# An attention and expert-layer kernel on one core: work dealt out anew over the engines in four stages

## The chip, the cores and the metric

The kernel runs on one core of one Trainium2 chip. A core has TensorE (PE) for matmuls, VectorE (DVE), ScalarE (ACT) and GpSimd (POOL) for everything elementwise, and SyncE (SP), which here issues transfers. Each engine runs its own list of instructions in order, and the lists meet only at semaphores. The metric is the device time of one execution in microseconds (us), and less is better. The kernel before takes 305.31 us, the median of 3 runs (305.03 to 306.4).

## The reference

There are 4 batches of 1024 tokens with 128 features each, 4096 tokens in all. A layer norm without weights, attention without learned projections, a second layer norm and a layer of 8 experts of which each token uses 2:

```python
x = x + attention(layernorm(x))        # lhs = h*w_lhs, rhs = h*w_rhs
                                       # scores = lhs @ rhs.T; softmax; @ h
h = layernorm(x)                       # 4096 x 128
probs = softmax(h @ router_w.T)        # 8 experts
topk_probs, topk_idx = top_k(probs, 2)
topk_probs = topk_probs / sum(topk_probs)
y = gelu(h @ w_fc[e] + b_fc[e])        # 128 -> 512, for the 2 experts of a token
y = y @ w_proj[e] + b_proj[e]          # 512 -> 128
out = x + sum over the 2 experts of topk_probs * y
```

## The kernel before

A batch of 1024 tokens is two units of 512 and 8 tiles of 128 tokens; batches have the indices 0 to 3. The order of the work is written out by hand in five lists, one for each engine, and what an engine waits for is a count on a semaphore. Nothing is scheduled by a planner.

**Prologue.** DVE takes the moments of the first two units, POOL makes the reciprocal deviation and the shift (`scale`, L785), ACT writes the normalised rows of unit 0 (`normalise`, L967) and DVE those of unit 1 (L1689). PE turns them with an identity (`turn_h`, L1137), after and before matmuls that compute nothing and only keep it busy (`stay_busy`, L1127). ACT copies the turned rows rounded to the matmul's format (`high_parts`), and DVE computes what the rounding lost (`low_parts`, L1448). The parts with and without the weights are called q and hT.

**Attention.** For each batch there are 16 blocks of 128x512 scores, each from three matmuls of high and low parts (`score`, L1152). DVE takes the largest value of each row (`row_max`, L1503), PE adds its negative into the block (`turn_negs` L1164, `shift_scores` L1170), ACT takes the exponent (`exponent`, L991; a block whose bank is wanted is first copied aside by `keep_again`, L989), and PE multiplies with the rows (`attend`, L1182). Scores of batch b are mixed with the last exponents and products of batch b-1. Beside that DVE adds the attention's result, takes moments for the second norm (`take_stats2`, `take_moments2`), chooses experts (`picks`, `find_gap`) and finds each token's place among its expert's rows (`keep_ranks`, `find_slots`); ACT and DVE make the normalised rows in two half-precision parts (`make_h2` and `high_h2` on ACT, `split_h2` on DVE, L1572). POOL sends them by indirect DMA into `slots`, a list in DRAM that is sorted by expert: 16 transfers for each batch (`dispatch`, L838 and L846).

**Passage.** When the first two batches are in `slots`, the first tiles of the experts start while the last batches are still chosen and sent. A table that says which expert a tile belongs to is computed in steps (`make_table`, L455). Experts' work is cut into 47 tiles: 24 of 256 rows and 23 of 128 rows. `ORDER` (L69) lists them in the order in which they run. At step k, SP loads tile k from `slots` (L723), PE turns the rows of a coming tile, does the up matmuls of tile k (L1366 to L1368) and the down matmuls of tile k-2 (L1387), ACT copies (`copy_xT`, L1086) and takes gelu (L1094), DVE adds the bias and multiplies by the gate for tile k-3 (`add_bias` L1872, `gate` L1880) and reads the row numbers of tile k (`keep_rows`, L842). The last round of ranks is a matmul too (`rank_round`, L1199), at step 4, after the bias of tile 1.

**End.** POOL sends each result to its token's place in `results` (`give_back`, L950). SP loads the first half of `results` when the tiles before `EARLY` have been sent, and the second half after all; DVE adds both results of each token to the row (L1913, L1915), and the output is stored, from ACT's queue for the first half (L1123) and from SP's for the second. `NB` is 8 buffers of tiles, `NH` is 4 buffers of row numbers and results, `FULL` is 24.

## Time and profile before

| what | value |
|---|---|
| median of the runs | 305.31 us |
| profiled execution, its own time | 305.57 us |
| its span in the trace | 304.0 us |
| PE busy | 269.3 us, 89% |
| DVE busy | 229.5 us, 75% |
| ACT busy | 196.4 us, 65% |
| POOL busy | 180.6 us, 59% |

The 1.57 us between the profiled execution's time and its span lie around the traced instructions. A busy PE is not a PE at its peak, since matmuls are pipelined and their ends are modelled; a share is a mean over stages with different limits, so a stage has to be read by itself. The stages in the trace are: prologue until 12.3 us, attention of the four batches until 153.2, the passage with the first tiles until 210, tiles with nothing else beside them until 281, and the end until 304.

### The profile page before, as it was taken

The numbers are of one execution on the slowest core, as the hardware profiler recorded it, in microseconds if no ns is written. First come the engines' busy times: TensorE is split into PE (matmuls) and PEld (weight loads), VectorE is DVE, ScalarE is ACT, GpSimd is POOL, SyncE is SP. The second block draws the span as 40 slices with busy tenths as digits, with TensorE's granted clock in tenths as the row PEclk, the third lists the DMA queues.
The fourth block names the chain that finished last, engine by engine and source line by source line (L and its number), as shares of the span: only waits on it lengthen the run. The fifth ranks groups of instructions, "written<-read, shape, count | busy, mean of one in ns | idle before, by whom it ended". The sixth has DMA issues, their size and how long they took to land.

```text
span 304.0 us, 8244 instructions
## 1 busy us (share of the span) xinstructions
PE 269.3 (89%) x2223; PEld 240.0 (79%) x2223; DVE 229.5 (75%) x1002; ACT 196.4 (65%) x427; POOL 180.6 (59%) x245
## 2 busy tenths in 40 slices
PE   7999999899999988899999699998999999999400
PEld 3589998789978977678888589987999999998400
DVE  4699898979878868988989777794565556666736
ACT  2447378897359772545679947774788788898200
POOL 8111036017667792687877657777777777777600
PEclk9999999999999999999999999999999999999955
DMA  6960000000401100111251143124233332221986
GB/s 195 412 293 4 0 3 0 3 0 0 144 27 57 37 27 11 37 45 38 69 140 63 38 118 109 55 73 125 73 97 100 95 93 82 81 73 55 352 279 248
DMA packets 15450, 28.51 MB, mean 94 GB/s; under 512 B 3904, under 2 KB 9920, under 8 KB 15152
## 3 DMA queue, kind: packets, MB, share of 16 engines
q1 hardware_dynamic: 10224, 16.88, 17.0%
q0 software_dynamic: 4608, 10.07, 9.9%
q10 hardware_dynamic: 576, 1.05, 1.0%
q8 instruction: 20, 0.33, 0.5%
q14 instruction: 22, 0.18, 0.2%
HBM read 15.83 MB, written 12.16 MB: 92 GB/s over the span
## 4 chain that ended last, share of the span: by engine, by line
PE 50%; POOL 14%; issue 13%; DVE 9%; DMA 7%; ACT 5%; SPq 1%; POOLq 0%; DVEq 0%; ACTq 0%
PE av_ps L1387 15%; PE av_ps L1182 11%; POOL slots L846 10%; PE sc_ps L1366 4%; PE sc_ps L1368 3%; PE sc_ps L1367 3%; DVE neg_piece L1503 3%; DMA raw_proj<-results 3%; DMA slots<-stage,slot 2%; DMA slots_in<-slots 2%; PE bank L1353 2%; PE sc_ps L1171 2%; PE bank L1158 1%; ACT h_all L972 1%; PE bank L1160 1%
## 5 line engine op out<-in xcount | busy, mean ns | idle before, releaser
L1094 ACT ACTIVATE raw_fc<-sc_ps,bfc,scale_down 128x128 f32<-128x128 f32 (+1 forms) x188 | 81.6, 530 | 0.7 <-PE sc_ps L1368 0.7
L950 POOL DMA_INDIRECT results<-prob,result_row x71 | 68.6, 967 | 22.1 <-issue 12.2
L846 POOL DMA_INDIRECT slots<-stage,slot x64 | 64.1, 1002 | 29.2 <-issue 18.9
L1387 PE MATMUL av_ps<-raw_proj,raw_fc 128*128 x568 | 72.7, 278 | 2.8 <-issue 1.9
L1182 PE MATMUL av_ps<-h_all,prob 128*128 128x137 f32 x512 | 73.2, 285 | 0.6 <-DVE lg_part L1534 0.4
L1387 PEld LDWEIGHTS av_ps<-raw_proj,raw_fc 128*128 128x128 f32 x568 | 67.0, 192 | 4.9 <-issue 4.5
L1182 PEld LDWEIGHTS av_ps<-h_all,prob 128*128 128x128 f32 x512 | 66.8, 190 | 4.4 <-DVE res L1531 1.6
L1366 PE MATMUL sc_ps<-h_all,wfc_hi 128*128 128x128 f16 (+1 forms) x188 | 43.2, 247 | 1.3 <-ACT raw_fc L1094 1.2
L1872 DVE TENSOR_TENSOR h_all<-av_ps,bpr 128x256 f32<-128x256 f32 (+1 forms) x47 | 16.9, 359 | 35.4 <-PE sc_ps L1368 31.8
L1368 PE MATMUL sc_ps<-h_all,wfc_lo 128*128 128x128 f16 (+1 forms) x188 | 43.1, 246 | 0.0
L1367 PE MATMUL sc_ps<-h_all,wfc_hi 128*128 128x128 f16 (+1 forms) x188 | 43.1, 246 | 0.0
L1086 ACT ACTIVATE h_all<-bank 128x512 f16<-128x512 f16 (+1 forms) x47 | 23.4, 501 | 25.2 <-PE sc_ps L1368 25.0
L1503 DVE TENSOR_REDUCE neg_piece<-bank 128x1 f32<-128x512 f32 x32 | 22.0, 687 | 7.3 <-PE sc_ps L1171 3.5
L999 ACT ACTIVATE prob<-sc_ps 128x512 f32<-128x512 f32 x32 | 18.1, 599 | 10.0 <-PE sc_ps L1171 9.9
L989 ACT ACTIVATE again<-bank 128x512 f32<-128x512 f32 x16 | 9.6, 597 | 21.9 <-DVE neg_piece L1503 21.9
L1503 DVE TENSOR_REDUCE neg_piece<-sc_ps 128x1 f32<-128x512 f32 x32 | 21.9, 684 | 1.1 <-PE sc_ps L1160 1.0
L1366 PEld LDWEIGHTS sc_ps<-h_all,wfc_hi 128*128 x188 | 18.4, 98 | 3.0 <-issue 1.8
L1880 DVE TENSOR_SCALAR prob<-h_all,row_gate 128x128 f32<-128x128 f32 x71 | 19.5, 301 | 1.4
L1368 PEld LDWEIGHTS sc_ps<-h_all,wfc_lo 128*128 x188 | 18.4, 98 | 1.1
L1367 PEld LDWEIGHTS sc_ps<-h_all,wfc_hi 128*128 x188 | 18.4, 98 | 0.8
L1353 PE MATMUL bank<-ident,slots_in 128*128 128x128 f16 x142 | 15.3, 219 | 2.2 <-DMA slots_in<-slots 2.2
L1009 ACT ACTIVATE h<-res,shift,rstd 128x128 f32<-128x128 f32 x32 | 14.4, 487 | 3.9 <-POOL shift L811 3.7
(201 smaller groups left out, 523.4 us busy)
## 6 DMA issues: line engine op xcount, KB each, us to landing
slots_in<-slots SPq DMA_DIRECT2D x24, 132.0 KB, 2.2
raw_fc<-in_w_fc_dram SPq DMA_DIRECT2D x1, 2048.0 KB, 11.3
raw_proj<-in_w_proj_dram SPq DMA_DIRECT2D x1, 2048.0 KB, 15.5
res<-in_x_dram SPq DMA_DIRECT2D x3, 512.0 KB, 5.9
slots_in<-slots SPq DMA_DIRECT2D x23, 66.0 KB, 1.8
results<-prob,result_row POOLq DMA_INDIRECT x71, 2.3
slots<-raw_fc POOLq DMA_DIRECT2D x2, 528.0 KB, 4.1
slots<-stage,slot POOLq DMA_INDIRECT x64
```

What stands on the lines that cost most here:

```text
L846: pool.indirect_dma_start(out=slots[:, :], out_offset=bass.IndirectOffsetOnAxis(ap=slot[:, n, k:k + 1], axis=0), in_=stage[:, b % 2, t, :] ...
L950: pool.indirect_dma_start(out=results[:, :], out_offset=bass.IndirectOffsetOnAxis(ap=result_row[a][:, h:h + 1], axis=0), in_=gated[a][h], ...
L1086: act.activation(xT[:, a % NH, 0:n], bank[a % 2][:, :].bitcast(F16)[:, 0:n], ACT.Copy).then_inc(xT_made, 1)
L1094: ins = act.activation(hid[:, a % NH, c, 0:halves_of(k) * P], up_ps(k, c), ACT.Gelu_apprx_tanh, bias=bfc[:, e, c:c + 1], scale=scale_down[ ...
L1182: mm = pe.matmul(att[:, t, 0:AUG], probT[:, m % RING, t * P:(t + 1) * P], h_aug[:, b % 2, exp_rows(n), :], start=(n % BT == 0 and t % 2 == ...
L1353: mm = pe.transpose(o[:, part * w + h * P:part * w + (h + 1) * P], x, ident16[:, :])
L1366: pe.matmul(o, wfc_hi[:, e, of], xT[:, a % NH, 0:w], start=True, stop=False, skip_group_check=True)
L1367: pe.matmul(o, wfc_hi[:, e, of], xT[:, a % NH, w:2 * w], start=False, stop=False, skip_group_check=True)
L1368: mm = pe.matmul(o, wfc_lo[:, e, of], xT[:, a % NH, 0:w], start=False, stop=True, skip_group_check=True)
L1387: mm = pe.matmul(o, hid[:, a % NH, c, rows], wpr[:, e, c, :], start=(c == 0 and h == 0), stop=(c == HC - 1), skip_group_check=True)
L1503: dve.tensor_reduce(neg_piece[:, r // TU, r % TU, c:c + 1], block_bank(n), AX_X, ALU.max, negate=True).then_inc(max_made, 1)
L1880: ins = dve.tensor_scalar(gated[k % NR][h], biased[:, a % NH, h, :], row_gate[:, a, h:h + 1], None, ALU.mult)
```

## The change

The same operations on the same data are dealt out anew in four stages, and a few are added.

Prologue: the rows of unit 0 are normalised by ACT (tiles 0, 1) and DVE (tiles 2, 3), those of unit 1 by POOL (tiles 0, 1, counted by `third_h_made`) and DVE (tiles 2, 3). POOL's first `scale` stands ahead of the constants that it makes by `affine_select`. PE issues 16 and 2 fillers instead of 20 and 8, turns every tile of the first two units a second time into another bank, and the low parts are computed from that one. The first scores wait for each operand apart.

Attention: `attend(b-1, 14)` is issued behind score 7 instead of behind score 4, and score 9 ahead of `shift_scores(1)` instead of behind it. In batch index 2, ACT's `make_h2` stands at exponents 10 and 11 instead of 6 and 7, and DVE does `find_slots(1)` and `add_logits` before the second `low_parts`, `keep_hrw(3)` before the moments, and `split_h2(3)` last.

Passage: DVE's steps of the table and of the choice of the last batch change places, `keep_ranks` and `find_slots` of the last batch come at step 4 instead of 5, and the moments of unit 6 are taken inside `find_slots`. PE does the last round of ranks at step 3 instead of 4, and waits for `ranks_kept` at step 2's place in the down matmuls instead of 3's. ACT's `make_h2` comes one by one, POOL's sequence of transfers, norms and the gate is cut differently.

End: the last tile of 256 rows runs as the 41st, not as the 38th, `EARLY` is 39 instead of 40, loads of tiles wait for one row count less, row numbers are read up to 4 tiles ahead in the later tiles, and `add_results(0)` stands inside the last step.

```diff
--- before.py
+++ after.py
-    for i in range(NB):
+    for i in range(NB - 1):
         ORDER.append(2 * NB + i)
         ORDER.extend(range(FULL + 2 * i, FULL + 2 * i + 2))
-    ORDER.extend(range(FULL + 2 * E, NTILES))
+    ORDER.extend(range(FULL + 2 * (NB - 1), FULL + 2 * E + 1))
+    ORDER.append(FULL - 1)
+    ORDER.extend(range(FULL + 2 * E + 1, NTILES))
...
-                    if k < NB + 3:
-                        sp.wait_ge(stepped, turned_at(k - NB))
-                    sp.wait_ge(row_made, k - NB + 2)
+                    sp.wait_ge(stepped, turned_at(k - NB))
+                    sp.wait_ge(row_made, k - NB + 1)
...
+            pool.wait_ge(consts, N_CONSTS - 2)
+            scale(0)
+            pool.affine_select(out=ident[:, :], in_=ident[:, :], compare_op=ALU.not_equal, fill=1.0,
+                               base=0, pattern=[[-1, P]], channel_multiplier=1).then_inc(ident_made, 1)
+            scale(1)
+            pool.wait_ge(shift_made, 2)
+            for t in range(2):
+                pool.tensor_scalar(h_aug[:, 0, TU + t, 0:D], res[:, token_tile(1, t), :], rstd[:, 1, t:t + 1], shift[:, 1, t:t + 1],
+                                   ALU.mult, ALU.add).then_inc(third_h_made, 1)
...
-                    if n >= BT - 2 and b >= 1:
+                    if n >= BT - 2 and b >= 1 and b != B - 2:
                         for t in (0, 1) if n == BT - 2 else (2, 3):
                             make_h2(2 * b - 1, t)
                         if n == BT - 1:
                             high_h2(2 * b - 1)
                 keep_rows(2 * b + 1)
                 for n in range(BT, EXPS):
+                    if n in (BT + 2, BT + 3) and b == B - 2:
+                        for t in (0, 1) if n == BT + 2 else (2, 3):
+                            make_h2(2 * b - 1, t)
+                        if n == BT + 3:
+                            high_h2(2 * b - 1)
                     if n == BT + 1 and b + 1 < B:
...
+                if k == 0:
+                    gelu(k, a)
                 if tile_there(k + 2):
                     copy_xT(k + 2, (a + 2) % NB)
-                if tile_there(k):
+                if 0 < k < NTILES:
                     gelu(k, a)
 
-                if k < 2:
-                    make_h2(2 * B - 2, 2 + k)
-                    if k == 1:
+                if k < 3:
+                    for t in range((0, 1, 3)[k], (1, 3, TU)[k]):
...
+                first = b == 0 and n < 2
+                if first:
+                    pe.wait_ge(hThi_made, c + 1)
+                    pe.wait_ge(qhi_made, 1)
+                if first and n == 1:
+                    pe.wait_ge(qlo_made, 1)
                 pe.matmul(o, q_hi[:, a, rows], hT_hi[:, a, cols], start=True, stop=False, skip_group_check=True)
+                if first:
+                    pe.wait_ge(hTlo_made, c + 1)
                 pe.matmul(o, q_hi[:, a, rows], hT_lo[:, a, cols], start=False, stop=False, skip_group_check=True)
+                if first:
+                    pe.wait_ge(qlo_made, 1)
                 mm = pe.matmul(o, q_lo[:, a, rows], hT_hi[:, a, cols], start=False, stop=True, skip_group_check=True)
...
+                else:
+                    parts_made(1)
...
-                if b >= 1:
-                    attend(b - 1, 14)
...
                 if b >= 1:
+                    attend(b - 1, 14)
                     attend(b - 1, 15)
...
                 shift_scores(0)
+                score(b, 9)
                 pe.wait_ge(max_made, maxed_at(b, 8))
                 shift_scores(1)
-                score(b, 9)
...
@@ -1375,7 +1418,7 @@
...
-                if k == 3:
+                if k == 2:
                     pe.wait_ge(ranks_kept, len(ROUNDS))
                 if k >= 2:
                     pe.wait_ge(biased_made, k - 1)
...
-                if k == 4:
-
-                    pe.wait_ge(biased_made, 2)
+                if k == 3:
+
+                    pe.wait_ge(biased_made, 1)
                     rank_round(len(ROUNDS) - 1)
...
-            dve.wait_ge(consts, N_CONSTS)
-            take_spread(0)
-            dve.wait_ge(shift_made, 2)
-            for t in range(TU):
-                dve.tensor_scalar(h_aug[:, 0, TU + t, 0:D], res[:, token_tile(1, t), :], rstd[:, 1, t:t + 1], shift[:, 1, t:t + 1],
-                                  ALU.mult, ALU.add).then_inc(second_h_made, 1)
+            dve.wait_ge(consts, N_CONSTS - 2)
+            for u in range(2):
+                dve.wait_ge(shift_made, u + 1)
+                for t in range(2, TU):
+                    dve.tensor_scalar(h_aug[:, 0, u * TU + t, 0:D], res[:, token_tile(u, t), :], rstd[:, u, t:t + 1], shift[:, u, t:t + 1],
+                                      ALU.mult, ALU.add).then_inc(second_h_made, 1)
+                if u == 0:
+                    take_spread(u)
+            low_parts(0)
+            low_hT(1)
             take_spread(1)
-            low_parts(0)
-            low_parts(1)
...
+                    if b == 0 and n == 0:
+                        low_q(1)
...
+                if b == B - 2:
+                    find_slots(b - 1)
+                    add_logits(2 * b)
...
-                    add_logits(2 * b)
+                    if b != B - 2:
+                        add_logits(2 * b)
                     if b == B - 2:
                         early = picks(ROUNDS_BY[b] - 2)
                         steps(early, 6)
                     row_max(b + 1, 0)
-                    take_stats2(2 * b)
+                    if b != B - 2:
+                        take_stats2(2 * b)
                     keep_hrw(b + 1)
+                    if b == B - 2:
+                        take_stats2(2 * b)
+                        split_h2(2 * b - 1)
...
-            STEPS = {0: second_table, 1: choose, 2: choose, 6: late_table, 7: late_table, 8: late_table, 9: late_table,
+            STEPS = {0: choose, 1: second_table, 2: second_table, 6: late_table, 7: late_table, 8: late_table, 9: late_table,
...
-            def step(k, a):
-
...
+            AHEAD = NH
+
+            def rows_by(k):
+
+                return min(NTILES, k + 1 + min(AHEAD, max(0, (k - FULL) // 2)))
+
+            def step(k, a):
+
+                if k == 0:
+                    def pick():
+                        steps(choose, 1)
+                    take_stats2(2 * B - 1, pick)
+                    take_moments2(2 * B - 1, pick)
+                if k == 4:
+                    split_h2(2 * B - 2)
+                    keep_ranks(last)
+                if 3 <= k < 6:
+                    add_bias(k - 3, (a - 3) % NB)
+                    gate(k - 3, (a - 3) % NB)
+                if k == 4:
+                    find_slots(last)
+                for j in range(rows_by(k - 1), rows_by(k)):
+                    keep_rows(j, j % NB)
+                if k >= 6:
+                    add_bias(k - 3, (a - 3) % NB)
+                    beside(k)
+                    gate(k - 3, (a - 3) % NB)
+                beside(k, {0: 30, 1: 6, 2: 40, 6: 3, 7: 3, 8: 3, 9: 40, 13: 40}.get(k, 3))
+                if k == NTILES - 1:
+                    add_results(0)
+                if k == 2:
+                    find_gap(last)
+                if k == 3 + TU:
+                    split_h2(2 * B - 1)
+            run_each_tile(load_experts, step, 3, lambda group: dve.wait_ge(table_made, group + 1))
+
```

What moves on the engines is listed from the two programs, a row for each instruction or run of like ones, with what it waits for.

PE in the prologue before; `busy` are the fillers, `h_all` the normalised rows, `sc_ps` and `bank` score banks:

```order
L1131 MATMUL av_ps<-busy 128x512 x19
L1142 MATMUL bank<-ident,h_all 128x128 [waits h_made,consts]
L1142 MATMUL bank<-ident,h_all 128x128 [waits h_made] x3
L1142 MATMUL bank<-ident,h_all 128x128 [waits second_h_made] x4
L1131 MATMUL av_ps<-busy 128x512 x8
L1158 MATMUL sc_ps<-hT_hi,q_hi 128x512 [waits hTlo_made,qlo_made,qhi_made,hThi_made]
L1159 MATMUL sc_ps<-hT_lo,q_hi 128x512
L1160 MATMUL sc_ps<-hT_hi,q_lo 128x512
```

The same place after the change:

```order
L1160 MATMUL av_ps<-busy 128x512 x15
L1172 MATMUL bank<-ident,h_all 128x128 [waits h_made,ident_made,consts]
L1172 MATMUL bank<-ident,h_all 128x128 [waits h_made]
L1172 MATMUL bank<-ident,h_all 128x128 [waits second_h_made] x2
L1176 MATMUL sc_ps<-ident,h_all 128x128 x4
L1160 MATMUL av_ps<-busy 128x512 x2
L1172 MATMUL bank<-ident,h_all 128x128 [waits third_h_made] x2
L1172 MATMUL bank<-ident,h_all 128x128 [waits second_h_made] x2
L1176 MATMUL sc_ps<-ident,h_all 128x128 x4
L1198 MATMUL sc_ps<-hT_hi,q_hi 128x512 [waits qhi_made,hThi_made]
L1201 MATMUL sc_ps<-hT_lo,q_hi 128x512 [waits hTlo_made]
L1204 MATMUL sc_ps<-hT_hi,q_lo 128x512 [waits qlo_made]
```

The fillers between the turns and the first score are gone, each unit is turned twice, and the waits of the first score stand at its three matmuls.

POOL at the passage before; `slots<-stage` are the transfers of batch index 2, `gate` the gates of the last batch, and the rows of `neg_mean`, `rstd` and `shift` the second norm of units 6 and 7:

```order
L846 DMA slots<-stage,slot 32768x132 [waits meta_made,h2lo_made] x6
L802 TENSOR_SCALAR neg_mean<-moments 128x4 [waits ln2_moments]
L808 TENSOR_TENSOR rstd<-var,minus_half 128x4 [waits gap_made,h2hi_made,ln2_var]
L811 TENSOR_TENSOR shift<-neg_mean,rstd 128x4 [waits ln2_mean,ln2_rstd]
L846 DMA slots<-stage,slot 32768x132 [waits meta_made,h2lo_made] x6
L802 TENSOR_SCALAR neg_mean<-moments 128x4 [waits ln2_moments]
L808 TENSOR_TENSOR rstd<-var,minus_half 128x4 [waits gap_made,h2hi_made,ln2_var]
L811 TENSOR_TENSOR shift<-neg_mean,rstd 128x4 [waits ln2_mean,ln2_rstd]
L846 DMA slots<-stage,slot 32768x132 [waits meta_made,h2lo_made] x3
L855 TENSOR_TENSOR gate<-euler,gap 128x8 [waits slots_made,gap_made]
L846 DMA slots<-stage,slot 32768x132 [waits meta_made,h2lo_made] x9
```

The same place after the change:

```order
L855 DMA slots<-stage,slot 32768x132 [waits meta_made,h2lo_made] x8
L811 TENSOR_SCALAR neg_mean<-moments 128x4 [waits ln2_moments]
L817 TENSOR_TENSOR rstd<-var,minus_half 128x4 [waits gap_made,h2hi_made,ln2_var]
L820 TENSOR_TENSOR shift<-neg_mean,rstd 128x4 [waits ln2_mean,ln2_rstd]
L855 DMA slots<-stage,slot 32768x132 [waits meta_made,h2lo_made] x3
L811 TENSOR_SCALAR neg_mean<-moments 128x4 [waits ln2_moments]
L817 TENSOR_TENSOR rstd<-var,minus_half 128x4 [waits gap_made,h2hi_made,ln2_var]
L820 TENSOR_TENSOR shift<-neg_mean,rstd 128x4 [waits ln2_mean,ln2_rstd]
L855 DMA slots<-stage,slot 32768x132 [waits meta_made,h2lo_made] x2
L864 TENSOR_TENSOR gate<-euler,gap 128x8 [waits slots_made,gap_made]
L855 DMA slots<-stage,slot 32768x132 [waits meta_made,h2lo_made] x11
```

The two norms stand after 8 and 11 transfers instead of 6 and 12, and the gate after 13 instead of 15, with 3 transfers of batch index 2 behind it where there was 1.

DVE at the passage before; `pick`, `taken`, `step_down` and `gap` belong to the choice of the last batch, `stage` is `split_h2(6)`, the last row shown is the first bias:

```order
L1607 SCALAR_TENSOR_TENSOR pick<-pick,expert_id 128x64 [waits route_chain]
L1859 SCALAR_TENSOR_TENSOR chosen_row<-slots_in,of_expert 128x2
L1611 TENSOR_REDUCE first_id<-pick 128x8 [waits route_chain]
L1863 TENSOR_TENSOR row_gate<-gate_parts 128x2 [waits row_parts]
L1614 TENSOR_TENSOR pick<-pick,first_id 128x64 [waits route_chain]
L1865 TENSOR_TENSOR result_row<-chosen_row,spare_row 128x2
L1622 TENSOR_TENSOR taken<-pick 128x2x32 [waits route_chain]
L1628 TENSOR_TENSOR step_down<-best 128x8
L1633 TENSOR_TENSOR gap<-step_down,rstd 128x8 [waits gate_exp,ln2_rstd,route_chain]
L1872 REGISTER_ALU [waits stepped]
L1872 ISA
L1872 TENSOR_TENSOR h_all<-av_ps,bpr 128x256
```

The same place after the change; `skipped`, `digits`, `used` and `tile_start` belong to the table:

```order
L591 TENSOR_TENSOR digits<-of_expert,digit 128x8
L595 TENSOR_TENSOR spare_row<-spare_row,spare 128x16 [waits dve_chain]
L597 TENSOR_REDUCE turn_number<-digits 128x1
L600 CAST turn_experts<-turn_number 128x1 [waits dve_chain]
L616 TENSOR_TENSOR capped<-capped 128x16 [waits dve_chain]
L620 TENSOR_TENSOR used<-used,capped 128x8 [waits dve_chain] x2
L623 SCALAR_TENSOR_TENSOR tile_start<-of_expert,tile_last 128x8 [waits dve_chain]
L1693 TENSOR_TENSOR step_down<-best 128x8
L1698 TENSOR_TENSOR gap<-step_down,rstd 128x8 [waits gate_exp,ln2_rstd,route_chain]
L1950 REGISTER_ALU [waits stepped]
L1950 ISA
L1950 TENSOR_TENSOR h_all<-av_ps,bpr 128x256
```

The choice stands ahead and the table's last steps stand directly before `gap`, and `split_h2(6)` has gone behind the first bias.

## Rows read from the trace of the kernel before

**Rows 1.** Windows, core 0: stretch, length, busy time (and count) of each engine, clock, DMA.

```profile
114.00:153.20 39.20, 35.53 (x241) 30.89 (x240) 35.59 (x156) 20.07 (x37) 26.23 (x30) 1.00 0.14 43
210.00:281.00 71.00, 70.84 (x787) 68.30 (x785) 42.24 (x231) 59.09 (x155) 53.91 (x57) 1.00 0.29 85
```

**Rows 2.** Timeline of PE in attention: start, length, what, [idle before <-releaser].

```profile
54.55 0.63 PE L1167 MATMUL bank<-ident,neg_cols 128*128 128x128 f32 x4 [0.55 <-ACT again L989]
...
56.65 0.50 PE L1171 MATMUL bank<-neg_rows,ones_r 128*128 128x512 f32 x1 [0.30 <-DVE neg_piece L1503]
...
107.71 0.50 PE L1171 MATMUL sc_ps<-neg_rows,ones_r 128*128 128x512 f32 x1 [0.99 <-ACT neg_rows L985]
...
121.18 0.50 PE L1158 MATMUL bank<-hT_hi,q_hi 128*128 128x512 f32 x1 [1.29 <-DVE h_all L1462]
...
127.95 0.63 PE L1167 MATMUL bank<-ident,neg_cols 128*128 128x128 f32 x4 [1.16 <-ACT again L989]
...
130.21 0.50 PE L1171 MATMUL bank<-neg_rows,ones_r 128*128 128x512 f32 x1 [0.45 <-DVE neg_piece L1503]
```

**Rows 3.** Timeline of ACT, batch index 2, the normalisation of the second norm.

```profile
103.16 0.88 ACT L1009 ACTIVATE h<-res,shift,rstd 128x128 f32<-128x128 f32 x2 [1.96 <-POOL shift L811]
```

**Rows 4.** Timeline of POOL: the prologue, and an elementwise operation later.

```profile
5.32 0.54 POOL L782 TENSOR_SCALAR_AFFINE_SELECT ident<-ident 128x128 f32<-128x128 f32 x2
...
7.12 0.20 POOL L797 TENSOR_TENSOR shift<-neg_mean,rstd 128x4 f32<-128x4 f32 x1
...
46.84 2.39 POOL L816 TENSOR_TENSOR wfc_lo<-raw_fc,wfc_hi 128x512 f16<-128x512 f32 x2 [1.49 <-ACT raw_fc L1025]
```

**Rows 5.** Timeline of ACT and DVE in the prologue.

```profile
7.36 1.65 ACT L972 ACTIVATE h_all<-res,shift,rstd 128x128 f32<-128x128 f32 x4 [1.63 <-POOL shift L797]
...
10.76 0.69 DVE L1454 TENSOR_TENSOR hT_lo<-bank,hT_hi 128x512 fp32r<-128x512 f32 x1 [0.81 <-ACT q_hi L981]
...
13.29 0.68 DVE L1503 TENSOR_REDUCE neg_piece<-sc_ps 128x1 f32<-128x512 f32 x1
```

**Rows 6.** Lines: the fillers L1131 in two stretches of the prologue.

```profile
L1131 PE MATMUL av_ps<-busy x11: 584/634/634, 1.5 to 5.8; 128*128 128x512 f16 x11
...
L1131 PE MATMUL av_ps<-busy x9: 379/379/584, 5.8 to 7.7; 128*128 128x512 f16 x9
```

**Rows 7.** Windows, after the last matmul: stretch, length, busy times, clock, DMA.

```profile
285.00:289.00 4.00, 0.00 (x0) 0.00 (x0) 3.79 (x8) 0.00 (x0) 2.84 (x3) 1.00 0.94 374
```

**Rows 8.** Timeline of DVE at the passage.

```profile
166.25 0.68 DVE L1572 TENSOR_TENSOR stage<-h,stage 128x512 f16<-128x512 f32 x1
...
168.41 0.17 DVE L1633 TENSOR_TENSOR gap<-step_down,rstd 128x8 f32<-128x8 f32 x1
168.64 0.42 DVE L1872 TENSOR_TENSOR h_all<-av_ps,bpr 128x256 f32<-128x256 f32 x1
```

**Rows 9.** Timeline of PE at the passage and in the early tiles.

```profile
169.30 2.05 PE L1387 MATMUL av_ps<-raw_proj,raw_fc 128*128 x16 [0.88 <-ACT raw_fc L1094]
...
174.90 2.05 PE L1387 MATMUL av_ps<-raw_proj,raw_fc 128*128 x16 [1.77 <-issue]
...
177.59 0.40 PE L1353 MATMUL bank<-ident,slots_in 128*128 128x128 f16 x4 [0.64 <-DMA slots_in<-slots]
...
206.32 0.40 PE L1353 MATMUL bank<-ident,slots_in 128*128 128x128 f16 x4 [1.59 <-DMA slots_in<-slots]
```

**Rows 10.** Timeline of POOL at the passage.

```profile
170.44 1.67 POOL L855 TENSOR_TENSOR gate<-euler,gap 128x8 f32<-128x8 f32 x1
172.31 1.03 POOL L846 DMA_INDIRECT slots<-stage,slot  x1 [0.19 <-issue]
177.15 0.95 POOL L846 DMA_INDIRECT slots<-stage,slot  x1 [3.81 <-DVE stage L1572]
```

**Rows 11.** Timeline of POOL and DVE at the end.

```profile
285.76 1.36 POOL L950 DMA_INDIRECT results<-prob,result_row  x1 [0.30 <-DVE prob L1880]
...
295.53 0.69 DVE L1913 TENSOR_TENSOR res<-res,raw_fc 128x512 f32<-128x512 f32 x1 [4.53 <-DMA raw_fc<-results]
```

143 lines of the change are left out of this document (78 added, 65 removed).

## The prediction

> **What bounds the kernel now.** I read the shares first: PE is busy 89% of the span, so a change that leaves PE's matmuls as they are can only win where PE waits. The windows by stage say where that is. From 210 to 281 PE is busy 70.84 of 71.00 us at a granted clock of 1.00 [rows 1]: rows read ahead on DVE and an earlier load buy nothing there. In batch index 3 PE has 35.53 and DVE 35.59 of 39.20 us [rows 1]: two engines nearly full, and whichever waits passes its wait on. Next I listed PE's idle time row by row, and followed each wait to the engine it names. What is left lies in four places: before the first score, in attention, at the passage, and behind the last matmul. All times below are in the frame of the trace of before.
>
> **A. Prologue.** The chain is shift, last normalised row, turn, copies, low parts, first maximum. Shift 0 ends at 7.32 (7.12 + 0.20), behind two rows of constants of 0.54 us that now stand after it [rows 4]: 6.78. ACT then makes two rows instead of four: 0.88 for two of such a kind [rows 3] against 1.65 for four [rows 5], with DVE's two beside them. The last row of unit 0 comes at 6.78 + 0.04 + 0.88 = 7.7 instead of 9.01. That is 1.3 us. A further wait goes: DVE's first low part waited 0.81 us for q [rows 5], though it needs only hT, and its first maximum stood behind four low parts at 13.29 [rows 5]; now three stand ahead of it and the fourth, 0.7 us, behind it. What is late next is unit 1: POOL makes two rows of it, an operation that no row shows. From below I take ACT's 0.44 for one, from above half of 2.39 for an elementwise POOL operation of four times the columns [rows 4], 1.2 us. I take 0.4, near ACT's, since the columns are the same; at 1.2 the two rows would be 1.6 us later than that and eat most of what is beyond the 0.9 that ACT's shorter chain gives score 0. The fourth low part now stands between the first and second maximum, so 0.7 of the 2.7 in sight is given back. A = -2.0, with ends -0.9 and -2.4.
>
> Here a port could matter. A transfer of POOL took 1.36 us while DVE added two operands, and 1.03 at another place [rows 10, 11]. The Trainium skill (SBUF — State Buffer, Who interferes with whom) says that DVE and GpSimd share one port pair as an exclusive lock, which the one that started first holds for its whole instruction, where DVE reads two operands there or runs in a two-port mode, as it can for a row of the norm. By that rule POOL's two rows would each stand behind one of DVE's two rows beside them, and A would be some 0.3 us less. The two rows do not settle it, and the sum goes without it.
>
> **B. Attention.** In batch index 1 PE waits 0.55 us before it turns the maxima and 0.30 before the second shift [rows 2]. The same two stand in batch index 2. Behind the change, four matmuls of `attend` (14) stand where the first wait was, and score 9 where the second was, both ready long before: -1.7 for the four. In batch index 2 the shift at 107.71 waits 0.99 for ACT, and ACT's row that makes it late waited 1.96 for POOL's shift [rows 2, 3]. That row moves behind, to exponents 10 and 11, and holds two products there by up to 0.88; I count 0.2. In batch index 3 the wait of 1.29 before score 3 is for `keep_hrw`, which now precedes the moments, and 1.16 and 0.45 follow [rows 2]. DVE stays as full as it was [rows 1], so part of it will come back ahead of scores 5 and 7, where PE waits for copies: I count 1.2 for the first two together and 0.45 for the third. B = 1.7 + 0.2 + 1.65 = -3.55. Ends: -1.5, if batch index 3 gives nothing and one pair comes back; -5.2, if every wait named goes.
>
> **C. Passage.** DVE runs without a gap up to the last batch's `gap` at 168.41 and the first bias at 168.64 [rows 8]. The choice and the table change places, the work is the same: `split_h2(6)`, 0.68 us [rows 8], leaves the stretch, and some ten rows that stood between others as cover now follow each other; each loses at most a row's 0.17 [rows 8], together 1.7. I take them as equal: `gap` and first bias where they were, 168.4 and 168.6, ends -0.7 and +1.0.
> PE ends the down matmuls of tile 1 at about 166.7 (169.30, less 0.88 of idle time, less 1.7 for turn and up of tile 4) [rows 9], up to 1.1 sooner since gelu 0 is first on ACT. There it now meets the rank round, which waits for the first bias: a pause of 2.6 to 3.7 us where it had 0.88 and 1.77 [rows 9], and behind the waiting matmul stand the up matmuls of tile 4. From 169.2 on PE does rank, up 4, down 2, up 5, down 3, 0.3 + 1.7 + 2.0 + 1.7 + 2.0, and comes to tile 8 at 176.9, as before (177.59 - 0.64) [rows 9].
> Tile 8 needs every transfer of batch index 2. On POOL the gate stood at 170.44 for 1.67 and one transfer behind it at 172.31 [rows 10]. Now POOL comes to the gate two transfers sooner, about 167.3, waits for `gap` until 168.5, and has three transfers behind it: 168.5 + 1.7 + 3 x 1.22 (1.03 and the 0.19 ahead of it [rows 10]) = 173.9 against 173.3. With 0.1 for the middle of `gap`'s two ends, tile 8's wait of 0.64 becomes 1.3: +0.7. In return ranks come a step sooner: POOL's idle 3.81 ahead of 177.15 [rows 10] goes, batch index 3 is sent some 2.5 us earlier, and the wait of 1.59 at tile 16 [rows 9] goes: -1.6. C = -0.9. Ends: -2.5, if tile 8's load is no later and its 0.64 goes too with the rest; +2.5, if `gap` is 1.0 late, POOL and tile 8 with it, and tile 16 still waits.
>
> **D. End.** The loads of the first half start sooner, by some 2 us as an estimate, since `EARLY` ends with a tile less, and a tile takes 1.5 to 2 us of PE's 71 [rows 1]. Two additions of it, 0.7 us each, now stand between the last gates, and POOL's last transfers wait for gates; the transfer at 285.76 waited for a gate already [rows 11]. The second half's additions waited 4.53 for its loads [rows 11], and these start after POOL's last transfer, so a gate that is held is paid in full. Against that, one store starts earlier and leaves the second half's loads freer. I take -0.3, ends -1.2 and +1.4.
>
> Sum: -2.0 - 3.55 - 0.9 - 0.3 = -6.75. The profiled execution took 305.57 us, 0.26 above the median of the runs: 305.57 - 6.75 = 298.8 us.
>
> **The rivals.**
> R1: attention's waits come back elsewhere. For it: in batch index 3 both engines are full [rows 1], and in batch index 2 ACT holds products. Against it: in batch indexes 1 and 2 the waits are short and what fills them is ready. B is then -1.0: 305.57 - 2.0 - 1.0 - 0.9 - 0.3 = 301.4.
> R2: the passage is late. The table's last steps, all in a chain, now stand directly before `gap`. If they cost the 1.0 more and tile 8 is 1.7 later, with tile 16 still free of its wait, C = +0.1 in place of -0.9; if tile 16 waits too, +1.7. I take +1.7: 301.4.
> R3: the clock falls. Ten fillers less stand in the prologue, a pause before the first score takes their place, and PE pauses up to 3.7 us at the rank round. The price: at the low level, 1.2 GHz, fillers stood 0.43 us apart ((5.8 - 1.5)/10), at the high one, 2.4 GHz, 0.24 ((7.7 - 5.8)/8) [rows 6]. A low stretch as long as that first one, 4.3 us, thus costs 1.9 us, and two cost 3.8: 302.6. Against it: four us without any matmul still had a granted clock of 1.00 [rows 7], longer than either pause. The Trainium skill (TensorE: Matmul & The Clock Gate, What's actually happening) says that the throttled state is the default and activity releases it; that leaves R3 open, and the row speaks against it.
> R4, slower: reading rows ahead. In the last 21 tiles DVE waits for a tile's load up to 4 tiles ahead of need, with the biases queued behind the wait and PE behind the biases. If the loads come no sooner, each of, say, 18 tiles costs 0.64, the smallest wait for a load that PE shows [rows 9]: 298.8 + 11.5 = 310.3; it decides from 11 tiles on. Against it: 8 buffers, so that a load is issued some 6 tiles ahead, and a PE without any wait for loads in that stretch [rows 1].
>
> **How the numbers follow.** Forecast 0.53 (its own range 297.0 to 300.6), R1 0.21, R2 0.13, R3 0.08, R4 0.05. All gains at their ends give 294.3, which I do not expect at once; two ends beyond the terms on the good side give 295.2, and R1, R2 and R3 reach to 302.8. A measurement of this kernel tells 0.5%, about 1.5 us, from no change. Faster than 303.8: forecast, R1, R2 and most of R3, less the case of several at once, 0.88; within the bound 0.06; slower 0.06.
>
> **What would show it.** A: first maximum near 11.2. B: no idle time before the turned maxima and the second shift in batch indexes 1 and 2; in batch index 3 the 1.29 gone, and smaller waits at scores 5 and 7. C: PE's longest pause of the passage at the rank round, POOL waiting before the last gate, no 3.81 before batch index 3, tile 8 waiting more, tile 16 not. D: two additions before the last gate. Wrong would be: a first maximum later than 12.4, a first bias after 169.6 in the frame of before, waits for loads on DVE after step 26, or a granted clock below 1.00 before the last matmul.

## The result, and the profile after

The changed kernel takes 301.98 us, the median of 4 runs (300.18 to 302.63), against 305.17 us before (4 runs): ratio 0.987, 95% interval 0.9838 to 0.9902. The forecast was 298.8 us. The time lies in the whole range that the prediction gave (295.2 to 302.8), but outside the forecast's own (297.0 to 300.6) and near the 301.4 of R1 and R2. The gain of 3.2 us is about half of the 6.75 forecast. The profiled execution took 302.37 us, with a span of 300.6.

The first answer is in the clock column. These are the windows of the changed kernel that answer to [rows 1], with the columns as there:

```profile
114.00:153.20 39.20, 37.19 (x235) 32.68 (x236) 34.78 (x153) 19.29 (x36) 26.93 (x31) 0.91 0.16 49
210.00:281.00 71.00, 70.91 (x789) 68.39 (x787) 44.48 (x232) 59.39 (x157) 53.91 (x57) 1.00 0.34 100
```

In batch index 3 PE is busier by 1.66 us than before with no more matmuls (235 rows against 241), at a clock of 0.91 in the place of 1.00: it works more slowly. The tiles from 210 to 281 are as they were. Cut finer, three stretches of the changed kernel stand at 0.50 to 0.51, half of the full clock, 1.2 GHz instead of 2.4. Such a stretch is called a fall below.

```profile
20.00:23.50 3.50, 3.50 (x10) 2.74 (x10) 2.76 (x14) 1.78 (x4) 2.47 (x5) 0.51 0.17 66
...
115.60:122.30 6.70, 6.70 (x25) 5.83 (x24) 4.85 (x21) 0.60 (x1) 1.91 (x3) 0.50 0.07 23
...
166.90:173.50 6.60, 5.66 (x36) 4.97 (x37) 4.50 (x23) 2.11 (x6) 4.80 (x4) 0.50 0.08 23
```

In the kernel before there is none ahead of the last matmul:

```profile
8.00:284.00 276.00, 262.05 (x2200) 236.96 (x2199) 214.19 (x961) 194.24 (x424) 170.32 (x194) 1.00 0.24 76
```

PE's timeline shows what stood ahead of two of them. The rows of [rows 2] at 54.55, 56.65, 107.71, 121.18, 127.95 and 130.21 have no counterpart any more: those waits are gone (in batch index 3 in part because PE itself is late there: low_first, which has no fall there, has waits again). New are two longer ones:

```profile
115.16 0.47 PE L1226 MATMUL av_ps<-h_all,prob 128*128 128x137 f32 x2 [1.75 <-DVE q_lo L1507]
...
167.84 0.25 PE L1250 MATMUL av_ps<-taken,before 128*128 128x80 f16 x1 [3.25 <-DVE h_all L1950]
```

The first pause, 1.75 us for DVE's low part of q, ends 0.4 us before the clock is down; the second, 3.25 us for the first bias, is the forecast's pause at the rank round. The stretch at 20 us has no such pause ahead of it, only the short matmuls of the routing.

Why was q's low part late? Timelines of POOL and DVE of the changed kernel, at the end of batch index 2:

```profile
108.56 3.38 POOL L825 TENSOR_TENSOR wfc_lo<-raw_fc,wfc_hi 128x512 f16<-128x512 f32 x3
```

```profile
109.01 3.02 DVE L1716 TENSOR_TENSOR pick<-pick,rank 128x64 f32<-128x64 f32 x1
...
114.16 0.74 DVE L1507 SCALAR_TENSOR_TENSOR q_lo<-bank,w_d,q_hi 128x512 fp32r<-128x512 f32 x1
```

`pick<-pick,rank` is the first operation of `find_slots(1)`, which the change moved ahead of the low parts. It lasts 3.02 us; the other rows of its line last about 0.2. It ends when POOL's three operations on the weights end, at 112. Both of DVE's operands lie in SBUF, and so do those that POOL reads.

The prologue, where the rows answer to [rows 4, 5] (POOL, ACT, DVE):

```profile
6.65 0.20 POOL L806 TENSOR_TENSOR shift<-neg_mean,rstd 128x4 f32<-128x4 f32 x1
...
8.66 0.94 POOL L900 TENSOR_SCALAR h_all<-res,rstd,shift 128x128 f32<-128x128 f32 x2
...
6.88 0.88 ACT L994 ACTIVATE h_all<-res,shift,rstd 128x128 f32<-128x128 f32 x2
...
11.55 0.68 DVE L1559 TENSOR_REDUCE neg_piece<-sc_ps 128x1 f32<-128x512 f32 x1
```

The shift ends at 6.85 (forecast 6.78), ACT's two rows at 7.76 (7.7), POOL's two take 0.47 each (0.4), and the first maximum starts 1.74 us sooner (13.29 before). The passage (DVE, POOL), which answers to [rows 8, 10]:

```profile
167.14 0.17 DVE L1698 TENSOR_TENSOR gap<-step_down,rstd 128x8 f32<-128x8 f32 x1
167.36 0.42 DVE L1950 TENSOR_TENSOR h_all<-av_ps,bpr 128x256 f32<-128x256 f32 x1
```

```profile
167.40 1.67 POOL L864 TENSOR_TENSOR gate<-euler,gap 128x8 f32<-128x8 f32 x1 [2.20 <-DVE gap L1698]
...
172.04 0.96 POOL L855 DMA_INDIRECT slots<-stage,slot  x1 [0.30 <-issue]
175.07 0.96 POOL L855 DMA_INDIRECT slots<-stage,slot  x1 [2.07 <-DVE stage L1739]
```

`gap` comes 1.3 us ahead of before, and attention was 1.4 us ahead at its end (its last products start at 146.11 instead of 147.55), so `gap` lost next to nothing; but POOL waits 2.20 us for it (1.2 forecast), and the last transfer of batch index 2 ends at 173.00 against 173.34. POOL's idle time before batch index 3 is 2.07 instead of 3.81. And the end, which answers to [rows 11]: POOL's last transfer, first before and then after the change, and DVE's first addition of the second half.

```profile
287.43 1.02 POOL L950 DMA_INDIRECT results<-prob,result_row  x1 [0.30 <-issue]
```

```profile
285.46 1.03 POOL L972 DMA_INDIRECT results<-prob,result_row  x1 [0.31 <-issue]
```

```profile
292.64 0.69 DVE L1965 TENSOR_TENSOR res<-res,raw_fc 128x512 f32<-128x512 f32 x1 [4.93 <-DMA raw_fc<-results]
```

### The profile page after: what moved, and what is told of

Same layout as the page of the kernel before. It is cut to its first block, busy times and chain, and to the rows that moved or that the text cites. A ratio compares the mean times of both kernels' runs of the same rounds, so it can differ in the third digit from the quotient of the medians.

```text
span 300.6 us, 8278 instructions
## 1 busy us (share of the span) xinstructions
PE 273.6 (91%) x2221; PEld 245.3 (82%) x2221; DVE 232.5 (77%) x1002; ACT 194.5 (65%) x425; POOL 181.3 (60%) x247
## 4 chain that ended last, share of the span: by engine, by line
PE 66%; DVE 21%; DMA 5%; issue 4%; POOL 2%; POOLq 0%; DVEq 0%; ACT 0%; SPq 0%
PE av_ps L1430 18%; PE av_ps L1226 15%; PE sc_ps L1409 5%; PE sc_ps L1411 4%; PE sc_ps L1410 4%; DVE neg_piece L1559 4%; PE bank L1396 2%; PE sc_ps L1215 2%; PE bank L1198 2%; PE sc_ps L1201 2%; PE sc_ps L1198 2%; PE sc_ps L1204 2%; PE bank L1204 2%; PE bank L1201 2%; DMA results<-prob,result_row 2%
## 5 line engine op out<-in xcount | busy, mean ns | idle before, releaser
L972 POOL DMA_INDIRECT results<-prob,result_row x71 | 69.7, 982 | 21.8 <-issue 14.9
L855 POOL DMA_INDIRECT slots<-stage,slot x64 | 62.7, 980 | 24.5 <-issue 17.8
L1226 PE MATMUL av_ps<-h_all,prob 128*128 128x137 f32 x512 | 74.3, 289 | 2.6 <-DVE q_lo L1507 1.7
L1430 PE MATMUL av_ps<-raw_proj,raw_fc 128*128 x568 | 73.8, 281 | 0.7 <-DVE h_all L1950 0.7
L1430 PEld LDWEIGHTS av_ps<-raw_proj,raw_fc 128*128 128x128 f32 x568 | 68.3, 195 | 2.1 <-issue 1.6
L1409 PE MATMUL sc_ps<-h_all,wfc_hi 128*128 128x128 f16 (+1 forms) x188 | 43.7, 250 | 0.0
L1410 PE MATMUL sc_ps<-h_all,wfc_hi 128*128 128x128 f16 (+1 forms) x188 | 43.6, 250 | 0.0
L1198 PE MATMUL bank<-hT_hi,q_hi 128*128 128x512 f32 x32 | 14.8, 463 | 0.0
## 6 DMA issues: line engine op xcount, KB each, us to landing
raw_fc<-in_w_fc_dram SPq DMA_DIRECT2D x1, 2048.0 KB, 11.2
```

Source lines behind the costliest of these rows:

```text
L855: pool.indirect_dma_start(out=slots[:, :], out_offset=bass.IndirectOffsetOnAxis(ap=slot[:, n, k:k + 1], axis=0), in_=stage[:, b % 2, t, :] ...
L972: pool.indirect_dma_start(out=results[:, :], out_offset=bass.IndirectOffsetOnAxis(ap=result_row[a][:, h:h + 1], axis=0), in_=gated[a][h], ...
L1198: pe.matmul(o, q_hi[:, a, rows], hT_hi[:, a, cols], start=True, stop=False, skip_group_check=True)
L1226: mm = pe.matmul(att[:, t, 0:AUG], probT[:, m % RING, t * P:(t + 1) * P], h_aug[:, b % 2, exp_rows(n), :], start=(n % BT == 0 and t % 2 == ...
L1409: pe.matmul(o, wfc_hi[:, e, of], xT[:, a % NH, 0:w], start=True, stop=False, skip_group_check=True)
L1410: pe.matmul(o, wfc_hi[:, e, of], xT[:, a % NH, w:2 * w], start=False, stop=False, skip_group_check=True)
```

## The experiments

All times are medians; the kernel before took 304.97 to 305.37 us beside them. The table has the times, the details stand below:

| run | us (runs) | ratio to before, 95% interval |
|---|---|---|
| again: changed kernel once more | 301.48 (4) | 0.9878, 0.9848 to 0.9907 |
| low_first | 299.81 (4) | 0.9842, 0.9803 to 0.9881 |
| bias_first | 299.44 (4) | 0.9799, 0.9763 to 0.9836 |
| pieces_later | 301.48 (4) | 0.9884, 0.9854 to 0.9915 |
| both | 297.16 (5) | 0.9744, 0.9720 to 0.9768 |
| both_gate | 297.08 (5) | 0.9737, 0.9711 to 0.9762 |
| all_fill | 296.25 (5) | 0.9719, 0.9693 to 0.9745 |
| end_before | 300.68 (4) | 0.9864, 0.9818 to 0.9910 |
| prologue_only | 302.81 (12) | 0.9938, 0.9918 to 0.9957 |
| attention_only | 303.53 (12) | 0.9955, 0.9931 to 0.9979 |
| late_split | 296.29 (5) | 0.9721, 0.9695 to 0.9747 |
| no_ahead | 300.58 (4) | 0.9845, 0.9812 to 0.9878 |

**again**: no edit.

> The changed kernel as it is, once more. Its first profile showed the granted clock below 1.00 in three places ahead of the last matmul: about 20 to 23.5 us, 115.6 to 122.2 and 167.9 to 174.1, each entered after a stretch in which PE had little to do, and its four runs had mean clocks of 0.948, 0.963, 0.969 and 0.951 with 302.37, 301.58, 300.18 and 302.63 us. Theory (the gains came as forecast, and falls of the clock gave some 3 us back): the time again goes with the mean clock, about 300 us at 0.970 and 302.5 at 0.950, and the falls at 115 and 168, which stand behind PE pauses of 1.75 and 3.25 us, are there again; the one at 20 may or may not be. Rival (falls anywhere, by chance, that any kernel of this length has): this profile has its falls at other places.

Its windows show one fall and not three. The second row is the fall; the first and third are places where the changed kernel's first profile had one:

```profile
20.00:23.50 3.50, 3.50 (x22) 3.06 (x22) 3.40 (x15) 2.79 (x7) 2.40 (x5) 1.00 0.12 47
113.90:120.60 6.70, 6.70 (x25) 5.93 (x24) 4.72 (x19) 0.60 (x1) 1.65 (x3) 0.50 0.07 23
163.00:173.00 10.00, 6.59 (x68) 5.74 (x67) 8.50 (x53) 6.03 (x14) 6.22 (x6) 1.00 0.11 36
```

So the fall behind the pause of 1.8 us came again; the one at 20 us did not, nor the one behind the rank round's pause of 3.22 us. The time did not follow the mean clock as closely as the theory said (301.29 us at 0.967, 301.45 at 0.952). PE's row for tile 8 shows why the fall at the passage is nearly free:

```profile
175.92 0.40 PE L1396 MATMUL bank<-ident,slots_in 128*128 128x128 f16 x4 [1.83 <-DMA slots_in<-slots]
```

Without the fall PE is early, and waits 1.83 us for the load. Attention ended 2.9 us ahead of the kernel before here and 1.4 us in the first profile; at tile 8 the lead is 1.7 here (175.92 against 177.59) and 0.1 there (177.46). They lose 1.2 and 1.3 us, without the fall and with it, and in both tile 8 stands 4.2 to 4.5 us behind POOL's last transfer of batch index 2: its load bounds it.

**low_first**, on the changed kernel:

```diff
-                if b == B - 2:
-                    find_slots(b - 1)
-                    add_logits(2 * b)
                 if b == 0:
                     take_stats(5)
                 if b + 1 < B:
                     low_parts(2 * b + 3)
+                if b == B - 2:
+                    find_slots(b - 1)
+                    add_logits(2 * b)
```

> In batch index 2 DVE does the second low parts ahead of find_slots and add_logits again, everything else as in the changed kernel. Theory (PE's pause of 1.75 us at 115.2 comes from DVE's first operation of find_slots, which lasted 3.02 us beside three elementwise operations of POOL that stood there for 3.38 us): low parts read score banks and do not wait for POOL, so they end near 112.6 instead of 114.9, the pause of PE before the last products of batch index 2 goes, the clock does not fall at 115, and the first shift of batch index 3, 0.9 us ahead of the kernel before, comes some 3 us sooner; the time is 1 to 3 us below the changed kernel. The long operation shrinks to 0.2 us, since POOL is done when it starts. Rival (the 3.02 us are a wait for something of its own, the ranks): the operation stays long where it now stands and DVE is late for the first maximum of batch index 3 by the same amount; no gain.

```profile
111.30 0.35 DVE L1716 TENSOR_TENSOR pick<-pick,rank 128x64 f32<-128x64 f32 x2
```

Two of the operations now take 0.35 us together (POOL's three ended at 110.57), the pause is gone and the clock stays at 1.00 there. The gain over the changed kernel is 1.7 us, as the theory said. PE's rows show what comes next, waits for copies of score blocks in batch index 3:

```profile
118.19 0.50 PE L1198 MATMUL bank<-hT_hi,q_hi 128*128 128x512 f32 x1 [1.20 <-ACT again L1011]
120.29 0.51 PE L1198 MATMUL bank<-hT_hi,q_hi 128*128 128x512 f32 x1 [0.46 <-ACT again L1011]
...
123.47 0.63 PE L1211 MATMUL bank<-ident,neg_cols 128*128 128x128 f32 x4 [0.33 <-ACT again L1011]
```

**pieces_later**, on the changed kernel, POOL's order alone:

```diff
-                    for i in range(EMPTY_PIECES, PIECES):
-                        low_part(i)
                     dispatch_own(b - 1, 0)
+                    for i in range(EMPTY_PIECES, PIECES):
+                        low_part(i)
```

> POOL does the three elementwise operations on the weights in batch index 2 behind the next two transfers instead of ahead of them; DVE's order is that of the changed kernel. Theory (a DVE operation with two operands in SBUF waits for POOL's elementwise operations beside it): the operation of 3.02 us shrinks to 0.2, low parts end near 112.6, PE's pause of 1.75 us goes, and instead another DVE operation with two such operands gets long where the three now stand; DVE operations that read a score bank beside them keep their length. Time between 3 us below the changed kernel and no change. Rival (a wait for the ranks): the operation stays at about 3 us.

```profile
112.38 3.39 POOL L825 TENSOR_TENSOR wfc_lo<-raw_fc,wfc_hi 128x512 f16<-128x512 f32 x3
```

```profile
110.50 0.74 DVE L1507 SCALAR_TENSOR_TENSOR q_lo<-bank,w_d,q_hi 128x512 fp32r<-128x512 f32 x1
...
112.09 3.73 DVE L1679 TENSOR_TENSOR pick<-pick,first_id 128x32 f32<-128x32 f32 x1
```

This decides it. The long row moved with POOL: `pick<-pick,rank` is short, and another operation with two SBUF operands, `pick<-pick,first_id`, about 0.2 us elsewhere, lasts 3.73 us beside POOL's three. The time is that of the changed kernel, since the stall only moved.

Yet the pause of 1.75 us and the fall behind it are gone here (PE now waits 1.70 us ahead of a score of batch index 3, at a clock of 1.00). So this run also tells the stall from the fall. PE turns the rows of the first tile, right behind attention, at these times in again (stall and fall), pieces_later (stall alone) and low_first (neither), three profiles without a fall at 20 us:

```profile
150.36 0.80 PE L1396 MATMUL bank<-ident,slots_in 128*128 128x128 f16 x8
```

```profile
149.92 0.73 PE L1396 MATMUL bank<-ident,slots_in 128*128 128x128 f16 x8
```

```profile
148.34 0.77 PE L1396 MATMUL bank<-ident,slots_in 128*128 128x128 f16 x8
```

As an estimate from these rows, the stall costs some 1.6 us (in its later place) and the fall at 115 some 0.4 on top.

The Trainium skill (SBUF — State Buffer, Who interferes with whom) says that a DVE instruction with two inputs in SBUF contends with a GpSimd instruction that reads SBUF, and one with at most a single SBUF input, outside the two-port modes, does not. The runs agree, with 3.02 and 3.73 us against 0.2, and so does the kernel before, where operations that read a score bank stood beside POOL's three and kept their 0.7 us.

**bias_first**, on the changed kernel, DVE at the passage:

```diff
-            STEPS = {0: choose, 1: second_table, 2: second_table, 6: late_table, ...
+            STEPS = {0: choose, 1: second_table, 2: second_table, 3: second_table, 4: second_table, 6: late_table, ...
...
-                    split_h2(2 * B - 2)
                     keep_ranks(last)
...
-                    find_slots(last)
+                    split_h2(2 * B - 2)
+                    find_slots(last, lambda: steps(second_table, 2))
...
-                beside(k, {0: 30, 1: 6, 2: 40, 6: 3, ...
+                beside(k, {0: 30, 1: 0, 2: 0, 3: 2, 4: 40, 6: 3, ...
```

> At the passage the second half of the table's steps stands behind the first bias on DVE instead of ahead of it, spread over steps 3 and 4; gap, the first bias, keep_ranks and find_slots of the last batch come sooner. Theory (PE's pause of 3.25 us before the last rank round waits for the first bias, which stands behind the table, and this pause lets the clock fall from 167.9 to 174.1): first bias about 3.5 us sooner, pause under 1 us, no fall behind it, POOL does not wait 2.2 us for gap, last transfer of batch index 2 some 2.5 us sooner, tile 8 then bound by its load at about 175 instead of 177; time 2 to 3 us below the changed kernel. Rival (the fall comes from short matmuls of the up stage, not from the pause): the fall stays near 168 to 174 and the gain is under 1 us. Second rival: the table, now finished only near 170 us, holds the load of tile 8, and the gain is nothing.

```profile
164.94 0.21 PE L1250 MATMUL av_ps<-taken,before 128*128 128x80 f16 x1 [0.26 <-DVE h_all L1950]
...
175.17 0.40 PE L1396 MATMUL bank<-ident,slots_in 128*128 128x128 f16 x4 [2.24 <-DMA slots_in<-slots]
```

```profile
165.23 1.67 POOL L864 TENSOR_TENSOR gate<-euler,gap 128x8 f32<-128x8 f32 x1
...
169.74 0.96 POOL L855 DMA_INDIRECT slots<-stage,slot  x1 [0.30 <-issue]
```

The pause is 0.26 us, POOL's gate follows its transfers without a wait, the last transfer ends at 170.70, 2.3 us sooner than in the changed kernel's first profile, and there is no fall at the passage (those at 20 and 115 us are there). The gain is 2.0 us. Tile 8 waits for its load, as expected.

**both**: the two edits together.

> The two edits of low_first and bias_first together on the changed kernel. Alone they came to 299.81 and 299.44 us against 301.48 of the changed kernel on the same chip, so 1.7 and 2.0 us. Theory (two separate places, each a DVE wait that PE passes on and a fall of the clock behind it): the gains add, 301.5 - 3.7 = 297.8 us; no granted clock below 1.00 between 30 us and the last matmul; tile 8 waits for its load. Rival (both only shorten the same chain, and the load of tile 8 bounds it): about 299.4, with PE's wait at tile 8 longer by what low_first gave.

297.16 us: the gains add. One part of the theory failed: the clock falls once more, at tile 8, where PE now waits 2.65 us for the load.

```profile
172.08 0.61 PE L1396 MATMUL bank<-ident,slots_in 128*128 128x128 f16 x4 [2.65 <-DMA slots_in<-slots]
```

```profile
171.80:175.00 3.20, 2.92 (x16) 2.18 (x17) 0.00 (x0) 0.00 (x0) 2.36 (x3) 0.51 0.66 170
```

**both_gate**, on both:

```diff
-            for i in range(11, 13):
-                dispatch(B - 2, i)
-            gate_powers(len(ROUNDS) - 1)
-            for i in range(13, SCATTERS):
+            for i in range(11, SCATTERS):
                 dispatch(B - 2, i)
+            gate_powers(len(ROUNDS) - 1)
```

> As both, and POOL computes the last gates behind all 16 transfers of batch index 2 instead of behind 13 of them. With bias_first alone PE waited 2.24 us for the load of tile 8, which needs the last of these transfers. Theory (that load is bound by POOL): the last transfer is issued 1.7 us sooner, the wait at tile 8 falls to about 0.6 us, the time is about 1.5 us below both, some 296.3. Rival (the last choice's slots now wait for the gates, batch index 3 is late, and tile 16 waits instead): no gain over both, and a wait for a load at tile 16.

```profile
170.75 0.40 PE L1394 MATMUL bank<-ident,slots_in 128*128 128x128 f16 x4 [1.19 <-DMA slots_in<-slots]
```

The wait at tile 8 is 1.19 us (2.65 in both), no wait comes at tile 16, and the profiled execution is 1.4 us shorter than that of both. The medians, 297.08 and 297.16, do not show it: both_gate's runs go from 295.66 at a mean clock of 0.977 to 297.75 at 0.966. Inconclusive by the medians.

**all_fill**, on both_gate: `stay_busy(2)` behind `route(0, range(5))`.

> As both_gate, with two matmuls that compute nothing behind the first five route matmul pairs of batch index 0, where PE waits 0.47 us. Of five profiles of the changed kernel and its variants two showed a low clock from about 20 to 23.5 us, right behind this stretch of short matmuls. Theory (the fall at 20 us comes from little activity before it, and fillers prevent it): no low clock at 20 us, and where both_gate's runs scatter by this fall, these scatter less; median 0 to 0.7 us below both_gate. Rival (the fall comes by chance whatever stands there): the same scatter of the mean clocks.

296.25 us, mean clocks 0.970 to 0.974 (both_gate: 0.966 to 0.977), no low clock at 20 us. Fewer low values, but the two medians lie within each other's runs; ten profiles with the new prologue and without the fillers show that fall twice, so whether fillers prevent it stays open. Its median is the lowest of all, 8.8 us below the kernel before, though not clear of both_gate and late_split.

**late_split**, on all_fill: `split_h2(3)` behind the seventh maximum of batch index 3.

> As all_fill, with DVE's split_h2(3) of batch index 3, 0.68 us, moved from behind keep_hrw to behind the seventh maximum. In all_fill PE waits 1.21, 0.44 and 0.35 us for copies of score blocks in batch index 3, and these copies wait for DVE's maxima. Theory (batch index 3 is bound by DVE's work between the first maxima): the three waits shrink by about 0.6 us in sum, median 0.6 us below all_fill's 296.25. Rival (DVE's work only moves, and the last maxima are as late as before): no difference.

```profile
117.50 0.49 PE L1196 MATMUL bank<-hT_hi,q_hi 128*128 128x512 f32 x1 [0.60 <-ACT again L1009]
119.61 0.50 PE L1196 MATMUL bank<-hT_hi,q_hi 128*128 128x512 f32 x1 [0.45 <-ACT again L1009]
...
123.39 0.63 PE L1209 MATMUL bank<-ident,neg_cols 128*128 128x128 f32 x4 [0.95 <-ACT again L1009]
```

The first wait falls from 1.21 to 0.60 us and the third rises from 0.35 to 0.95, and the three together stay at 2.0: the rival. DVE's work there only moves.

**end_before**, on the changed kernel: `ORDER`, `EARLY` and the first additions as in the kernel before.

> The changed kernel with the end of the kernel before: order of the last tiles, EARLY 40, and the first additions behind the last step; rows still read up to 4 tiles ahead. In the two profiles the end gave 1.4 us (last bias 2.0 us ahead of the kernel before, end of span 3.4 ahead), where 0.3 was forecast. Theory (the earlier first loads and stores leave the second half's loads freer): about 1.4 us above the changed kernel, 302.9 us, with the loads of the second half landing 5.5 us after their issue instead of 4.6. Rival (the 1.4 us are scatter of the transfers at the end): no difference, 301.5.

```profile
284.52 1.02 POOL L970 DMA_INDIRECT results<-prob,result_row  x1 [0.30 <-issue]
```

```profile
291.04 0.69 DVE L1963 TENSOR_TENSOR res<-res,raw_fc 128x512 f32<-128x512 f32 x1 [2.94 <-DMA raw_fc<-results]
```

From POOL's last transfer to the end of the span it takes 15.1 us (299.6 - 284.52), and 15.1 in the changed kernel (300.6 - 285.46). The rival holds as far as the time goes: this part of the change is worth nothing that shows. But the profiles show two effects against each other and not only scatter. Behind POOL's last transfer the four profiles with the old end take 15.1 to 17.4 us, the ten with the new one 14.5 to 15.7. Ahead of it, in eight of these ten, the first additions hold the last biases, and PE's last product waits 0.7 to 1.9 us for one; in the four with the old end it waits for none. In again DVE waits for the loads of the first half, and PE for DVE:

```profile
279.61 0.69 DVE L1965 TENSOR_TENSOR res<-res,hT_hi 128x512 f32<-128x512 f32 x1 [1.76 <-DMA hT_hi<-results]
```

```profile
281.47 1.15 PE L1430 MATMUL av_ps<-raw_proj,raw_fc 128*128 x8 [1.90 <-DVE h_all L1950]
```

POOL's last transfer starts 2.65 us behind PE's last product in all ten, so such a wait moves it by as much.

**no_ahead**, on the changed kernel: `AHEAD = 0`.

> The changed kernel with row numbers read at their own step in all tiles, not up to 4 tiles ahead. The forecast counted them as worth nothing since PE is busy 70.84 of 71.00 us in that stretch of the kernel before; a rival said that reading ahead makes DVE wait for loads. Theory: no difference, 301.5 us, PE busy over 70.8 of 71 us in either. Rival: some 1 us off, either way, at the last tiles, where gates hold POOL's last transfers.

300.58 us (299.38 to 302.43) against 301.48 and 301.98: no loss without it, so nothing that shows is gained by reading rows ahead.

**prologue_only**, the kernel before with that part:

> The kernel before with the prologue of the changed kernel alone. Forecast for this part: 2.0 us less. Measured in the profiles of the changed kernel: maxima of batch index 0 come 1.75 us sooner, and in the profiles with a low clock at 20 us 1.4 of it are lost again. Theory: 305.1 - 1.75 = 303.3 us in executions without that fall and 304.7 in those with it, a median between. Rival (the later parts of the kernel before are bound by DVE and by transfers and swallow it): 305.1, no difference.

302.81 us, 2.2 below before, at full clock up to the last matmul in the profile:

```profile
8.00:280.00 272.00, 259.23 (x2186) 235.02 (x2185) 212.96 (x956) 192.18 (x419) 169.98 (x197) 1.00 0.24 75
```

In this profile the part's lead over the kernel before is 1.6 us at the first maximum (11.68 against 13.29) and 1.5 at tile 8 (176.09 against 177.59). At tile 16 it is 3.5, because PE's wait of 1.59 us there [rows 9] is missing:

```profile
182.00:205.00 23.00, 23.00 (x223) 21.80 (x223) 19.19 (x113) 16.53 (x35) 17.51 (x19) 1.00 0.25 76
```

**attention_only**, the kernel before with that part:

> The kernel before with the moves in attention alone, on PE, ACT and DVE, prologue, passage and end as before. Forecast for this part: 3.55 us less. Theory now (PE's waits in batch indexes 1 and 2 go, some 2 us; then DVE's first operation of find_slots meets POOL's elementwise operations, lasts over 2 us, PE waits 1.75 us and the clock falls behind it): some 1 us less, 304.0 us, with a low clock for 6 to 7 us from about 117 us on. Rival (attention's moves gain what was forecast, and the loss in the changed kernel comes from its other parts): 301.5.

```profile
109.33 3.16 DVE L1655 TENSOR_TENSOR pick<-pick,rank 128x64 f32<-128x64 f32 x2
```

```profile
115.49 0.47 PE L1187 MATMUL av_ps<-h_all,prob 128*128 128x137 f32 x2 [1.75 <-DVE q_lo L1459]
```

```profile
116.90:120.90 4.00, 4.00 (x14) 3.37 (x15) 3.14 (x16) 0.46 (x1) 0.21 (x2) 0.57 0.06 18
```

303.53 us, 1.4 below before; the long operations (two in 3.16 us), the pause and the fall are there without any other part of the change. Its twelve runs go with the mean clock: four with 0.967 to 0.974 took 302.30 to 302.61 us, five from 0.959 to 0.963 took 303.78 to 304.90, and three at 0.964 and 0.965, the profiled one among them, lie between. Some 2 us go with the clock here. Where the others' clocks were low is not on record, and the rows under pieces_later give the fall at 115 some 0.4 us, so the 2 us are not shown to be the price of that fall.

This run also corrects the passage. It has the passage of before, as prologue_only has, and yet tile 16's wait of 1.59 us [rows 9] is gone in both:

```profile
182.00:210.00 28.00, 27.94 (x268) 26.54 (x268) 22.33 (x127) 20.62 (x44) 21.30 (x23) 1.00 0.28 82
```

Nothing on POOL explains it: ahead of batch index 3 it idles 3.81 and 3.79 us in these two, as before (3.81 [rows 10]). What differs is how long SP's load of tile 16 waited for the transfers: 11.2 us in the one profile of the kernel before, 10.0 in prologue_only and 9.7 here. So the 1.59 us look like scatter of transfers in one profile. A second profile of the kernel before would tell; there is none.

## Why the prediction was half right

**Prologue, forecast -2.0.** Right in mechanism, and the number in part by luck: -2.2 alone, and each step of the chain within 0.1 us but the first maximum (11.55, not 11.2). By that maximum the chain gives 1.6 to 1.8 us, and 1.5 are left at tile 8; the rest of the 2.2 does not show in the chain, and in prologue_only's profile further lead comes only with tile 16's missing wait. POOL's two rows took 0.47 us each beside DVE's, near the 0.4 forecast, so no wait for the shared port shows here.

**Attention, forecast -3.55.** Wrong in size: -1.4 alone. The failed step is the one that had no price: DVE's new order in batch index 2. I took PE's filled waits, which did go, and counted the moved `find_slots` at nothing, as the same work elsewhere. It is not, since its first operation has two SBUF operands, and its new place lies beside 3.38 us of POOL's work on the weights; in the old place DVE read score banks beside these. The stall of 2.8 us became PE's pause of 1.75, and a fall of the clock followed. Without the stall (low_first) 1.7 us come back, which as an estimate makes the part some -3.1. I weighed the port's rule at the prologue, where it did nothing, and not here, where it decided. The trace of the kernel before had a case of it: `x_logits`, with two SBUF operands, lasts 0.51 us at 47.57, beside POOL's operations on the weights [rows 4], and 0.22 or 0.23 at its three other places.

**Passage, forecast -0.9.** About nothing: the whole change is 3.2 to 3.9 us below before (two sets of runs), and prologue and attention alone are 2.2 and 1.4, which leaves -0.3 to +0.4 for passage and end together, if the parts add. The price was right in kind: tile 8 is later by POOL's wait for `gap`, 1.2 to 1.3 us instead of 0.7. The gain, -1.6 at tile 16, was not the passage's: that wait goes without it, as prologue_only and attention_only show, and is most likely scatter of the one profile that the prediction read.

**End, forecast -0.3; rows ahead, forecast nothing.** end_before and no_ahead show no loss without them. The hold that the forecast feared is there, up to 1.9 us ahead of POOL's last transfer, and the time behind it tends to be shorter; no run shows that their sum differs from nothing.

**The rivals.** R3, with 0.08, is what happened beside the forecast; a clock below 1.00 ahead of the last matmul was also one of the prediction's signs of being wrong. My argument against it was four us without a matmul at a clock of 1.00 [rows 7]. That row stands behind 70 us of dense matmuls, and I read it as a rule for any pause. It was also cut short: the same trace goes on at half the clock.

```profile
289.00:304.00 15.00, 0.00 (x0) 0.00 (x0) 7.41 (x11) 0.00 (x0) 0.00 (x0) 0.52 0.77 267
```

A pause of 1.75 us among short matmuls was followed by a fall in all six profiles that have it (the changed kernel, again, bias_first, end_before, no_ahead, attention_only), and one of 2.8 to 3.4 us at the rank round in five of six. Against that, a pause of 1.70 us ahead of a score (pieces_later) and waits of up to 2.24 us at tile 8 (bias_first) were followed by none; the one of 2.65 us at tile 8 (both) was followed by a fall. What about the stretch decides is not settled by these runs. The Trainium skill (TensorE: Matmul & The Clock Gate, What's actually happening) calls the throttled state the default, which activity releases; the traces agree in that the clock, each time it came back, did so in the course of unbroken matmuls.

R3's price of 1.9 us was read from the pace of the fillers, since the clock column stands at 1.00 in that first stretch too. The fall at 20 us bears the pace out, with matmuls of 512 columns 0.43 us apart at a clock of 0.51. But what a fall costs depended on what bounds its stage. By estimates from the rows, the one at 20 us cost some 1.4 (first tile at 151.79 with it, 150.36 in again without it), the longer one at 115 some 0.4, and the one at the passage next to nothing, since tile 8 waits for its load anyway.

R1 is true in part: with the stall gone (low_first), waits of 1.20, 0.46 and 0.33 us stand in batch index 3 where 1.29, 1.16 and 0.45 stood [rows 2]. R2's mechanism, POOL behind `gap`, is the passage's loss. R4 did not occur. The ends of the range were added a little wide (two ends beyond their terms give 295.6, and R3 reaches 302.6); nothing hangs on it.

With the two DVE orders mended (both), the change gives 297.16 us, a gain of 7.9 where 6.75 was forecast, though by other terms than the sum had.

## What to carry to other kernels

Work that is moved on DVE has a price that depends on what POOL does at its new place: look at the operands (two in SBUF, or one in a score bank) before counting it as the same work. When many short waits are filled and one longer one is left, ask what TensorE does in that stretch as a whole, and read the clock by stretches first in any profile whose busy time grew while the work did not. What a fall costs depends on whether TensorE bounds the stage. And a wait that a part is said to remove should be looked for in a version without that part, and in a second profile of the same kernel.

## What the runs showed of the hardware

A DVE operation of 0.2 us lasted 3.02 and 3.73 us beside three POOL operations of 3.4 us in sum: there it waited for all three, not for the first alone, and in pieces_later its row begins even 0.29 us ahead of POOL's. It is not always so long. In the kernel before, the first of POOL's two operations in [rows 4] runs from 46.84 to 48.01 and the second starts at 48.07. `x_logits` ends at 48.08, so it waited for the first and not for the second:

```profile
47.57 0.51 DVE L1467 TENSOR_TENSOR x_logits<-h_all,spread 128x64 f32<-128x64 f32 x1
```

Why it got in there and not at the three is open. Falls of the clock differ between executions of the same program: the changed kernel showed three in one profile and one in another, with mean clocks from 0.948 to 0.969 in its first four runs.
